# Mixture of experts in a decoder kernel: down products with the weights held still, token weights inside the up operand, all experts summed in PSUM

## The reference

```python
x_flat = x.reshape(-1, h)                       # 896 tokens, h = 128
logits = x_flat @ gate_w.T                      # 8 experts
top_v, top_i = jax.lax.top_k(logits, 2)
probs = softmax(top_v)
combine = einsum('tk,tke->et', probs, one_hot(top_i, 8))
def body(acc, ws):                              # for each of the 8 experts
    wge, wue, wde, we = ws                      # inner width 512
    hidden = silu(x_flat @ wge.T) * (x_flat @ wue.T)
    return acc + we[:, None] * (hidden @ wde.T), None
```

## Time and profile before

| | us |
|---|---|
| median of 3 runs (lowest to highest) | 647.84 (647.13 to 648.02) |
| profiled execution, its own time | 653.12 |
| its span, first to last instruction | 651.3 |
| PE busy | 593.1, 91% of the span |
| DVE busy | 427.2, 66% |
| ACT busy | 338.2, 52% |
| POOL busy | 183.2, 28% |

### The profile page before, as it was taken

How to read it: one execution, slowest core, us unless ns; L and a number is a source line. 1 busy time by engine, 2 the same in 40 slices (tenths; PEclk the granted TensorE clock), 3 DMA queues, 4 the chain that set the end, 5 groups by cost and what they waited for, 6 DMA issues and landing times. The chain is left out here.

```text
span 651.3 us, 17561 instructions
## 1 busy us (share of the span) xinstructions
PE 593.1 (91%) x6732; PEld 481.7 (74%) x6732; DVE 427.2 (66%) x799; ACT 338.2 (52%) x506; POOL 183.2 (28%) x149
## 2 busy tenths in 40 slices
PE   3799787798999999999999999999985699999997
PEld 1566374376877877877877787787774589999997
DVE  4765357866887788778788788877822464444443
ACT  2466445274666576567566566657564353333321
POOL 4685305622223323224223232322100221111100
PEclk9789789798999999999999999999998599999999
DMA  5000006498267356446536736734620011111100
GB/s 211 1 3 3 0 3 133 94 193 192 68 132 183 96 140 144 119 117 142 144 92 141 172 88 127 179 100 91 144 100 1 17 46 49 48 48 48 48 17 29
DMA packets 26190, 60.29 MB, mean 93 GB/s; under 512 B 14368, under 2 KB 15392, under 8 KB 26152
## 3 DMA queue, kind: packets, MB, share of 16 engines
q1 hardware_dynamic: 26152, 59.77, 38.3%
HBM read 20.48 MB, written 0.46 MB: 32 GB/s over the span
## 5 line engine op out<-in xcount | busy, mean ns | idle before, releaser
L1163 DVE TENSOR_REDUCE chunk_max<-PS 128x1 f32<-128x500 f32 x336 | 214.3, 673 | 62.2 <-PE PS L1283 60.5
L1103 ACT ACTIVATE P<-PS 125x896 f32<-125x896 f32 x192 | 173.3, 913 | 124.1 <-PE PS L1307 123.4
L1283 PE MATMUL PS<-k_hi,q_block_hi 128*128 128x500 f32 x336 | 131.3, 438 | 6.5 <-ACT k_full L246 3.3
L1307 PE MATMUL PS<-q_stack,k_stack 97*125 97x224 f32 x768 | 122.5, 283 | 4.3 <-DMA q_stack<-neg_rows 2.4
L1307 PEld LDWEIGHTS PS<-q_stack,k_stack 97*125 97x125 f32 x768 | 106.9, 190 | 19.3 <-issue 8.9
L255 POOL TENSOR_TENSOR k_lo<-k_full,k_hi 128x500 fp32r<-128x500 f32 x48 | 61.1, 1276 | 104.7 <-ACT k_full L246 102.4
L1283 PEld LDWEIGHTS PS<-k_hi,q_block_hi 128*128 128x128 f32 x336 | 60.9, 193 | 37.1 <-ACT k_full L246 16.7
L1629 DVE TENSOR_TENSOR hidden<-gated,PS 128x448 f32<-128x448 f32 x64 | 39.6, 619 | 69.2 <-PE PS L1686 63.8
L1323 PE MATMUL PS<-P,values 125*32 125x112 f32 x3072 | 84.4, 262 | 0.6 <-ACT P L1103 0.5
L1323 PEld LDWEIGHTS PS<-P,values 125*32 125x32 f32 x3072 | 72.6, 110 | 14.3 <-issue 10.8
L1541 ACT ACTIVATE gated<-PS 128x448 f32<-128x448 f32 x64 | 34.8, 544 | 80.5 <-PE PS L1686 76.0
(11 more groups left out here) (153 smaller groups left out, 666.7 us busy)
## 6 DMA issues: line engine op xcount, KB each, us to landing
k_stack<-k_hi SPq DMA_DIRECT2D x128, 187.5 KB, 4.5
ctxT<-ctx_in SPq DMA_DIRECT2D x16, 750.0 KB, 4.3
k_stack<-k_lo SPq DMA_DIRECT2D x64, 187.5 KB, 4.4
w_gate_up<-wgu_in SPq DMA_DIRECT2D x8, 512.0 KB, 3.7
w_down<-wd_in SPq DMA_DIRECT2D x8, 256.0 KB, 2.7
q_stack<-neg_rows SPq DMA_DIRECT2D x112, 0.5 KB
mats<-mats_in SPq DMA_DIRECT2D x1, 832.0 KB, 5.2
q_copies<-q_hi SPq DMA_DIRECT2D x8, 98.0 KB, 4.4
```

What stands on the lines that cost most here:

```text
L1103: nc.scalar.activation(P[:, t % RING, :].rearrange("p (a n) -> p a n", a=2), PS[0:KR, 2 * (t % 2):2 * (t % 2) + 2, 0:HALF], ACT.Exp).then_ ...
L1163: nc.vector.tensor_reduce(out=chunk_max[:, n // KC, n % KC:n % KC + 1], in_=PS[:, max_bank(b, n), 0:KW], axis=AX.X, op=ALU.max).then_inc(m ...
L1283: nc.tensor.matmul(PS[:, max_bank(b, n), 0:KW], q_block_hi[:, j, 128 * t:128 * t + 128], k_hi[:, j, KW * c:KW * c + KW], start=True, stop= ...
L1307: last = nc.tensor.matmul(PS[0:KR, 2 * (t % 2) + g // 2, o:o + GH * N], k_stack[:, j, g, KR * t:KR * t + KR], q_stack[0:SHIFT_ROW + 1, j, ...
```

## The change

Only the third stage changes.

- **Down.** The down weights are split too (`d_hi` by ACT, `d_lo` by POOL, 512 columns each) and become the still operand. The hidden activations are split and move: `round_hidden` on ACT (`hid_hi`) and `split_hidden` on DVE (`hid_lo`), in a ring of four. A down unit is three passes of 448 columns. All 8 experts and 4 tiles add up in two PSUM banks, 6 and 7; no result is read before the last expert.
- **Token weights.** They multiply the up product's input instead of the output. For each expert and half a spread product (16 rows by 448 columns, one pass) copies the weight row to all partitions, DVE multiplies it with `T3` (`weigh_tokens`, `xw`), ACT rounds (`round_weighted`), POOL takes the rest (`split_weighted`).
- **Multiply.** It writes back into the up bank in PSUM, of which there are four (2 to 5).
- **Order.** Gates run one expert ahead. Before up(e, k) PE does down(k - 3) and then gate(e + 1, k). Gates and spreads of an expert share banks 0 and 1 in the order of `MIXED`, each released by the reader of the one two places before.
- **Front.** The routing is done in one piece on DVE on tiles of 112 tokens, beside the eight gates of expert 0. Its weights are split, turned on PE, and copied to SBUF by ACT; then the two spreads follow.
- **End.** The sum is copied to SBUF by ACT, turned by fp32 products, added to `X` by DVE and written out in two DMAs. `X3`, the 22 copies, `weight_now` and `add_outputs` are gone.
- Loads of expert e + 2 wait for `down_split` of expert e.

```diff
+FRONT = [("gate", k) for k in range(UNITS)] + [("spread", 0), ("spread", 1)]
+MIXED = [("gate", 0), ("gate", 1), ("spread", 0), ("gate", 2), ("gate", 3), ("gate", 4), ("spread", 1),
+         ("gate", 5), ("gate", 6), ("gate", 7)]
...
+def front_released(e, order, i):
+    kind, n = order[i]
+    return (gated_ready, UNITS * e + n + 1) if kind == "gate" else (xw_ready, 2 * e + n + 1)
+def up_bank(k):
+    return PS[:, 2 + k % RING3, 0:HALF]
...
+            if exists(e + 2, E):
+                sp.wait_ge(down_split, e + 1)
+                load_gate_up(sp, e + 2, j)
+                load_down(sp, e + 2, j)
...
+        split_gate_up(0, 0, 0, gate_rounded, gate_split)
+        nc.gpsimd.memset(outT[:, :, N:PITCH], 0.0).then_inc(out_cleared, 1)
+        split_gate_up(0, 0, 1, up_rounded, up_split)
+        split_gate_up(1, 1, 0, gate_rounded, gate_split)
+        for c in range(2):
+            split_weighted(0, 0, c)
+        split_down(0, 0)
+            if exists(e + 1, E):
+                split_gate_up(e + 1, 1 - j, 1, up_rounded, up_split)
+                split_weighted(e + 1, 1 - j, 0)
+                split_down(e + 1, 1 - j)
+            if exists(e + 2, E):
+                split_gate_up(e + 2, j, 0, gate_rounded, gate_split)
+            if exists(e + 1, E):
+                split_weighted(e + 1, 1 - j, 1)
+        pipelined(pool, period, E)
...
+        def round_hidden(e, k):
+            act.wait_ge(hidden_ready, UNITS * e + k + 1)
+            if later(e, 1) or k >= RING3:
+                act.wait_ge(down_done, UNITS * e + k - RING3 + 1)
+            nc.scalar.copy(hid_hi[:, k % RING3, :], up_bank(k)).then_inc(hidden_rounded, 1)
...
+        act.wait_ge(route_shifted, 1)
+        nc.scalar.activation(weight[:, :, :], weight[:, :, :], ACT.Exp).then_inc(route_exp, 1)
...
+        for k in range(UNITS):
+            silu(0, FRONT, k)
...
+                round_hidden(e, k)
+                if exists(e + 1, E):
+                    silu(e + 1, MIXED, k)
+                    if k == 0:
+                        round_gate_up(e + 1, 1 - j, u if j == 0 else u + 1, 1, up_rounded)
+                    if k == 3:
+                        round_weighted(e + 1, 1 - j, 0)
+                    if k == 4:
+                        act.wait_ge(down_done, UNITS * e)
+                        round_down(e + 1, 1 - j, u if j == 0 else u + 1)
+                    if k == 7:
+                        round_weighted(e + 1, 1 - j, 1)
+                if k == 5 and exists(e + 2, E):
+                    round_gate_up(e + 2, j, u + 1, 0, gate_rounded)
...
+        def multiply(e, k):
+            dve.wait_ge(gated_ready, UNITS * e + k + 1)
+            dve.wait_ge(up_done, UNITS * e + k + 1)
+            nc.vector.tensor_tensor(up_bank(k), gated[:, k, :], up_bank(k), ALU.mult).then_inc(hidden_ready, 1)
...
+                multiply(e, k)
+                if k >= 1:
+                    split_hidden(e, k - 1)
+                elif later(e, 1):
+                    split_hidden(e - 1, UNITS - 1)
+                if exists(e + 1, E):
+                    if k in (2, 5):
+                        weigh_tokens(e + 1, MIXED, (2, 5).index(k))
+                if k == 6 and exists(e + 2, E):
+                    pick(e + 2, j)
...
+        def front(e, j, order, i):
+            kind, n = order[i]
+            if i >= 2:
+                pe.wait_ge(*front_released(e, order, i - 2))
+            elif later(e, 1):
+                pe.wait_ge(*front_released(e - 1, FRONT if isinstance(e, int) and e == 1 else MIXED,
+                                           len(order) + i - 2))
+            bank = PS[:, i % 2, 0:HALF]
+            if kind == "spread":
...
+        def up(e, j, k):
+            c, t = k // IT, k % IT
+            if k == 0:
+                pe.wait_ge(up_split, e + 1)
+            if t == 0:
+                pe.wait_ge(xw_split, 2 * e + c + 1)
+            if later(e, 1) or k >= RING3:
+                pe.wait_ge(hidden_split, UNITS * e + k - RING3 + 1)
+            w = slice(128 * t, 128 * t + 128)
+            three_passes(up_bank(k), w_hi[:, j, 1, w], w_lo[:, j, 1, w], xw_hi[:, j, c, :], xw_lo[:, j, c, :]
+                         ).then_inc(up_done, 1)
+        def down(e, j, k, first=False, final=False):
+            c, t = k // IT, k % IT
+            if k == 0:
+                pe.wait_ge(down_split, e + 1)
+            pe.wait_ge(hidden_split, UNITS * e + k + 1)
+            three_passes(PS[:, 6 + c, 0:HALF], d_hi[:, j, t, :], d_lo[:, j, t, :],
+                         hid_hi[:, k % RING3, :], hid_lo[:, k % RING3, :], first and t == 0,
+                         final and t == IT - 1, skip_group_check=True).then_inc(down_done, 1)
...
+                if k >= LAG:
+                    down(e, j, k - LAG, start, stop)
+                elif later(e, 1):
+                    down(e - 1, 1 - j, UNITS + k - LAG, isinstance(e, int) and e == 1)
+                if exists(e + 1, E):
+                    while MIXED[turn] != ("gate", k):
+                        front(e + 1, 1 - j, MIXED, turn)
+                        turn += 1
+                    front(e + 1, 1 - j, MIXED, turn)
+                    turn += 1
+                up(e, j, k)
+        pipelined(pe, period, E)
+        def turn_out(c):
+            pe.wait_ge(out_copied, c + 1)
+            if c == 0:
+                pe.wait_ge(gated_ready, UNITS * E)
+            for b in range(8 * c, 8 * c + 8):
+                p = b // 2 % 4
+                last = nc.tensor.matmul(PS[PITCH * (b % 2):PITCH * (b % 2) + PITCH, c, 128 * p:128 * p + 128],
+                                        outT[:, b, :], C["ident"], start=True, stop=True)
+            last.then_inc(out_turned, 1)
+        for k in range(UNITS - LAG, UNITS):
+            down(E - 1, 1, k, False, True)
+            if k == UNITS - LAG:
+                turn_out(0)
+        turn_out(1)
```

More of the change, by code:

```diff
@@ L1479, in _ @@
                 def _(sp):
[L1480 to L1483, removed]
                     def period(e, j, u):
[L1486 to L1493, removed]
@@ L1537, in period @@
                         for k in range(UNITS):
[L1538 to L1545, removed]
@@ L1637, in _ @@
-                    experts(dve, period)
-                    for half in range(2):
-                        add_outputs(E - 1, 1, half)
+                            multiply(e, k)
[6 more added lines that the diff above has]
+                                    weigh_tokens(e + 1, MIXED, (2, 5).index(k))
@@ new lines, in period @@
+                            if k == 6 and exists(e + 2, E):
+                                pick(e + 2, j)
+                    pipelined(dve, period, E)
+                    split_hidden(E - 1, UNITS - 1)
+                    for c in range(2):
+                        dve.wait_ge(out_turned, c + 1)
+                        part = X[:, HP * c:HP * c + HP, :]
+                        nc.vector.tensor_tensor(part, part, PS[:, c, :].rearrange("p (a d) -> p a d", d=D), ALU.add
+                                                ).then_inc(summed, 1)
@@ new lines, in _ @@
+                    for c in range(2):
+                        pe.wait_ge(t_split, c + 1)
+                        for k in range(IT * c, IT * c + IT):
+                            front(0, 0, FRONT, k)
+                    pe.wait_ge(weights_ready, 1)
+                    for c in range(2):
+                        for p in range(HP):
+                            last = nc.tensor.matmul(PS[0:2 * E, 4 + c, PT * p:PT * p + PT],
+                                                    weight_parts[:, HP * c + p, :].bitcast(F32), C["ident"][0:PT, 0:PT],
+                                                    start=True, stop=True)
+                        last.then_inc(weights_turned, 1)
@@ L1690, in _ @@
-                    experts(pe, period)
-                    down_turn[0] = E // 2 - 1
-                    for p in range(TT):
-                        down(E - 1, 1, p)
+                            if k >= LAG:
[8 more added lines that the diff above has]
+                                turn += 1
@@ L1736 @@
     got = run_bass_kernel_spmd(nc, [arrays], core_ids=[0]).results[0]["out"]
-    return np.ascontiguousarray(got.transpose(1, 0, 2)).reshape(B, N, D)
+    halves = [got[PITCH * e:PITCH * e + N] for e in range(2)]
+    return np.ascontiguousarray(np.stack(halves, axis=0).transpose(2, 0, 1, 3)).reshape(B, N, D)
```

329 lines of the change are left out of this document (171 added, 158 removed).

## The result

| | before | after |
|---|---|---|
| median of 4 runs, us | 647.93 | 694.91 |
| lowest to highest | 647.13 to 648.08 | 690.83 to 698.59 |
| ratio to before, 95% interval | | 1.0719 (1.0658 to 1.0779) |
| profiled execution, span | 653.12, 651.3 | 690.83, 689.0 |

The change costs 47 us; 42.7 were forecast (690.5, range 673 to 713). The profiled execution of after is the fastest of its four runs and that of before (653.12) is slower than all four in the table, so the spans are best compared from the moment when both token copies are there (start of the routing products): before 512.5 to 651.3, 138.8 us; after 505.3 to 689.0, 183.7 us. The two stages ahead of that point are the same code, and their length differs from trace to trace (505.3 to 512.5 us in the eleven traces of this study).

A forecast was written before the change was run, and what follows sets the result against it. PE was taken to bound the stage. 528.0 (first up product) + 1.5 clock + 142.5 periods + 10.5 last expert + 7.9 + 1.0 + 2.9 end = 694.3 us in the trace, scaled to 690.5; range 673 to 713.

The forecast's parts named there:

- The period: Each expert with a next one: PE work 14.95 us plus waits and restarts 5.5, 20.5 us against 15.93 before.
- The two waits: PE idle before gates 2 and 5 for silu, 1.15 us, and before gates 3 and 6 for xw, 1.41 us.
- PE's own work: Per expert: 72 passes of 0.202 us plus two spreads, 0.40 together, make 14.95 us, 1.0 less than before.
- Rival (c): Banks come free in time and the period is PE's own 14.95 us; 655.8 us in the trace, chance 0.06.
- The front: Token copies to first up product: routing, gates of expert 0, then a chain; from 512.5 us to 528.0 us.
- The clock behind it: Clock falling once around the first up product, where PE has little work; 1.5 us added.
- Rival (a): The clock falls in the periods too, a third of them at 1.2 GHz; 716 us, chance 0.07.
- The last expert: No gates beside it and split_hidden behind the next multiply: 1.42 us a unit, 10.5 us for eight.
- The end: After the last up product: down products, output copies and turns 7.9 us, sum 1.0, write out 2.9.
- The scaling by 0.8%: Whole trace forecast scaled because the profiled execution was 0.8% slower than the runs: 43.0 us more became 42.7, giving 690.5.
- (b): Waits in the periods are about half of those counted, 2.7 us a period instead of 5.5; 671 us, chance 0.05.
- (d): Hand-overs between engines cost next to nothing, so no bank is late; 645.1 us in the runs, chance 0.04.

The follow-up runs named there:

- both_first: Against after: both order edits, weigh_tokens ahead of multiply on DVE and silu ahead of round_hidden on ACT; median 657.1 us, 1.0138 of before.
- weigh_first: Against after: DVE takes weigh_tokens ahead of its unit's multiply instead of behind split_hidden; median 671.5 us, 1.0334 of before.
- silu_first: Against after: ACT takes the next expert's silu ahead of round_hidden, gated gets a second buffer, outT lies over T; median 677.0 us, 1.0431 of before.
- after_k128: Against after: spread products get 128 rows instead of 16, the added ones zero, order unchanged; median 690.7 us, 1.0626 of before.
- warm_front: Against after: 13 extra passes of 448 columns into an unread PSUM bank in PE's front waits; median 690.9 us, 1.0648 of before.
- tuned2: Against both_first: 128-row spreads, shorter front and end, last expert's down products lagging four units instead of three; median 646.3 us, 0.9969 of before.

## Why the prediction was right

- **The period.** "A period is 14.95 + 5.5 = 20.5 us": 20.62. The two waits were put at 1.15 and 1.41; the slots give 1.12 (569.67 to 570.79) and 1.41 (572.72 to 574.13). Some 0.2 of the 1.12 is the spread's own, which keeps the next pass back for 0.40 and not 0.20 (both_first). weigh_first and silu_first show that each wait comes from the order of one queue: each edit removed the waits it was aimed at and left the other kind in place. More than two banks for gates and spreads, the other way to remove them, was not tried.
- **PE's own work: a wrong term under a right sum.** "Two spread products of one pass each are added, 0.40": they cost 1.2 when nothing covers them. PE's own period is 15.87 (both_first), not 14.95. The step that failed is that the spread was priced like any other pass, though its 16 rows stood in the diff. That it didn't show in the time is luck: after waits for silu behind every spread, and that wait covers it (after_k128: no change of the period). So most of the 1 us for each expert that the new down passes seemed to give back was taken by the two spreads: with every wait gone the new period is as long as the old one, and only with spreads of 128 rows 0.8 shorter (15.10). Rival (c) at 655.8 in the trace would have needed the 14.95.
- **The front.** First up product 15.5 us after the token copies forecast, 16.6 measured (505.27 to 521.86). The chain after the last gate was 4.8 instead of 4.6; the rest is the clock, which rose 9.9 us after the copies and not 8.0.
- **The clock behind it.** One fall, 1.5 us, was in the sum; there were two, with 10.2 us at the low clock in all. From the first up product to that of the last expert I had 144.0, measured 147.1 (521.86 to 668.98). warm_front and after_k128, whose clock held, take 143.3 and 143.1, so the two falls cost about 4 us. Of the 3.1 too little some 2.4 are the clock, the rest is the periods, a little longer than 20.5. Rival (a) was so right for one period and wrong for the others in this trace: from 536 us on the clock stays at 1.00 with PE waiting four times in each period. By the Trainium skill, "TensorE: Matmul & The Clock Gate", section "A second HAM failure mode: psum-queue depth-cycling", cited in the prediction, it should have gone on swinging between its levels; it did so only around the first period, and the measurement decides. The trace is that of the fastest run of after. In the slowest (698.6 us) the mean clock over the whole execution was 0.948 against 0.965, and where it was low has no trace; before's runs differ in the same way (0.953 at 654.0 us and 0.973 at 646.8, beside weigh_first), so it need not be in this stage.
- **The last expert.** 1.42 a unit forecast, 1.44 measured (668.98 to 679.09 for seven). tuned2 shows the reason that was given: one more unit of lag brings 1.21.
- **The end.** From the end of the last up product 11.8 forecast (7.9 + 1.0 + 2.9), 9.3 measured. Some 1.5 to 1.7 of it is the turns, which were mis-sized: 8 products with 64 columns held still, 16 instructions, take 1.09 us and not 1.8 at 0.223 each (that price is from products with 128). Another 0.5 is the write out, 2.4 us after DVE's last operation (686.63 to 689.0) and not 2.9, the saving by halves that was left out of the sum:

```profile
684.21 0.53 ACT L1614 COPY outT<-PS 128x448 f32<-128x448 f32 x1 [2.60 <-PE PS L1732]
...
684.80 1.09 PE L1816 MATMUL PS<-consts,outT 128*64 128x128 f32 x16 [0.62 <-ACT outT L1614]
685.94 0.69 DVE L1713 TENSOR_TENSOR X<-X,PS 128x512 f32<-128x512 f32 x1 [2.45 <-PE PS L1816]
```

- **The sum.** In the stage 181.8 forecast, 183.7 measured: front +1.1, clock and periods +3.1, last expert +0.2, end -2.5. That it comes within 1.9 is partly luck, since the end was wrong the other way. The scaling by 0.8% then made 42.7 of the 43.0 and with it 690.5. It was the wrong tool: the two stages ahead of the change are the same code, and the trace of before reached the third stage at 512.5 us, the latest of the eleven traces, so that a fixed amount was to be taken off and not a share; 0.8% of 43 us is too little to matter here. The remaining 4.4 us to the median of 694.9 are within after's own scatter.
- **The chances.** Rivals (b), (c) and (d) are out by the pitch, which they put at 17.7, 14.95 and 14.95. (d), a hand-over at next to nothing, would have shown in the timeline as a gate starting before its releaser ended.

## What to carry to other kernels

Before work is moved to another form because its sum on the busiest engine is smaller, write down for each shared buffer who frees it and what stands ahead of that reader in its own queue: here two banks freed behind other work cost 5 us of 20, and changing the order of two queues (with a second buffer for `gated`) gave 38 of the 47 us back. A small product among full ones is not cheap by its size: compare the distances between starts around it, and try it with all 128 rows. When an edit of one's own seems to have held the clock up, look for a kernel without the edit whose clock held too. A cost that lies under a wait is worth nothing to remove until the wait is gone, so measure again after each one.

## What the runs showed of the hardware

- A pass of 448 columns whose still operand has 16 or 64 rows, between passes with 128, costs 0.60 us instead of 0.20: distances of 0.29, 0.40 and 0.30. Its weight load starts with the pass and not a slot ahead. Filled up with zeros to 128 rows it costs 0.20.
- A DVE product of 448 columns that writes to PSUM (L1685 of after) takes 0.629 us, the one that writes to SBUF (L1629 of before) 0.619.
- The granted clock (1.00 is 2.4 GHz, 0.50 is 1.2 GHz) fell twice around the first period of after and not in warm_front nor in after_k128, and in the one trace of after it never fell in the later periods, though PE waited there four times in each 20.6 us. What sets the cases apart was not settled.
